# Second half's queries in two quarters that share one bank, and two key products next to the couples' loop

## The reference

```python
x = x + tanh(g_xattn[0]) * L0_xattn(layernorm(x), ctx, ctx)     # a decaying running sum
x = x + tanh(g_ffn[0])   * L0_ffn(layernorm(x), ...)            # 8 experts, 512 wide, 2 chosen
x = x + tanh(g_xattn[1]) * L1_xattn(layernorm(x), ctx, ...)     # 16 heads of 8, rotary, with biases
x = x + tanh(g_ffn[1])   * L1_ffn(layernorm(x), ...)            # 8 gated experts, 352 wide
x = x + tanh(g_xattn[2]) * L2_xattn(layernorm(x), ctx, ...)     # tanh(query + key) for all pairs, softmax
x = x + tanh(g_ffn[2])   * L2_ffn(layernorm(x), ...)            # 16 gated experts, 128 wide, 4 chosen
x = x + tanh(g_xattn[3]) * L3_xattn(layernorm(x), ctx, ctx)     # 16 heads of 8, rotary
x = x + tanh(g_ffn[3])   * L3_ffn(layernorm(x), ...)            # 8 experts and a shared one, 512 wide
```

## Time and profile before

| | us |
|---|---|
| median of three runs | 596.08 |
| the three runs | 593.05, 596.08, 596.30 |
| the profiled execution | 593.17 |
| its span, first to last instruction | 591.4 |
| TensorE busy in it | 559.5 (95%) |
| VectorE busy | 440.1 (74%) |
| ScalarE busy | 402.6 (68%) |
| GpSimd busy | 101.9 (17%) |

### The profile page before, as it was taken

How to read it: one execution, slowest core, us unless ns; L and a number is a source line. 1 busy time by engine, 2 the same in 40 slices (tenths; PEclk the granted TensorE clock), 3 DMA queues, 4 the chain that set the end, 5 groups by cost and what they waited for, 6 DMA issues and landing times.

```text
span 591.4 us, 8708 instructions
## 1 busy us (share of the span) xinstructions
PE 559.5 (95%) x3251; PEld 385.4 (65%) x3256; DVE 440.1 (74%) x684; ACT 402.6 (68%) x559; POOL 101.9 (17%) x69
## 2 busy tenths in 40 slices
PE   7999999889999999999996989999998999999997
PEld 5688887656777867764331437566545767888886
DVE  4378987678648799977789775766767838787786
ACT  4799899756746645426999865534504858888875
POOL 5400000000110000004989713100000310000000
PEclk9999999999999999999899899999999999999999
DMA  6208110300100559200000024406410110712100
GB/s 241 65 11 319 54 54 1 116 1 2 55 1 2 190 197 245 71 29 1 7 1 1 1 71 126 162 3 170 151 35 1 38 38 2 319 40 70 36 2 35
DMA packets 19342, 43.81 MB, mean 74 GB/s; under 512 B 2090, under 2 KB 7594, under 8 KB 19300
## 3 DMA queue, kind: packets, MB, share of 16 engines
q1 hardware_dynamic: 19300, 43.25, 22.8%
HBM read 42.55 MB, written 0.70 MB: 73 GB/s over the span
## 4 chain that ended last, share of the span: by engine, by line
PE 73%; DVE 14%; ACT 8%; issue 3%; POOL 1%; DVEq 0%; ACTq 0%; POOLq 0%
PE ps L801 36%; ACT work L1197 5%; PE ps L843 4%; PE ps L783 3%; PE ps L557 3%; PE ps L540 3%; DVE h_lo L1729 2%; PE ps L827 2%; PE ps L672 2%; PE ps L829 2%; PE ps L643 2%; PE ps L828 2%; PE ps L868 2%; PE ps L547 2%; PE ps L657 2%
## 5 line engine op out<-in xcount | busy, mean ns | idle before, releaser
L1729 DVE TENSOR_TENSOR h_lo<-h_act,h_hi 128x512 fp32r<-128x512 f32 (+1 forms) x114 | 103.5, 912 | 39.9 <-ACT h_hi L1244 39.1
L801 PE MATMUL ps<-n_hi,w_hi 128*128 128x512 f32 x224 | 86.5, 421 | 2.4 <-DVE h_act L1702 1.2
L1244 ACT CAST h_hi<-h_act 128x1024 fp32r<-128x1024 f32 (+1 forms) x88 | 75.3, 856 | 14.7 <-PE ps L801 12.1
L801 PE MATMUL ps<-n_hi,w_lo 128*128 128x512 f32 x224 | 79.7, 391 | 0.0
L801 PE MATMUL ps<-n_lo,w_hi 128*128 128x512 f32 x224 | 79.7, 390 | 0.0
L1943 POOL TENSOR_TENSOR rstd<-var_eps,minus_half 128x4 f32<-128x4 f32 x16 | 17.1, 1070 | 313.6 <-DVE var_eps L1389 313.6
L1197 ACT ACTIVATE work<-work,p_rest 128x2048 f32<-128x2048 f32 x31 | 59.4, 1995 | 0.4 <-DVE work L1582 0.4
L1237 ACT ACTIVATE h_act<-ps 128x512 f32<-128x512 f32 x44 | 26.3, 597 | 45.5 <-PE ps L801 45.2
L801 PE MATMUL ps<-h_hi,w_hi 128*128 128x512 f32 x162 | 56.3, 396 | 0.1
L801 PE MATMUL ps<-h_hi,w_lo 128*128 128x512 f32 x162 | 55.4, 390 | 0.0
L801 PE MATMUL ps<-h_lo,w_hi 128*128 128x512 f32 x162 | 55.4, 390 | 0.0
(11 more groups left out here) (239 smaller groups left out, 1036.0 us busy)
## 6 DMA issues: line engine op xcount, KB each, us to landing
work<-g_rows SPq DMA_DIRECT2D x36, 512.0 KB, 5.8
w_f<-in_w SPq DMA_DIRECT2D x20, 512.0 KB, 3.6
w_f<-in_w SPq DMA_DIRECT2D x8, 384.0 KB, 3.3
work<-g_rows SPq DMA_DIRECT2D x8, 256.0 KB, 6.9
work<-g_rows SPq DMA_DIRECT2D x4, 384.0 KB, 7.2
diag<-in_w SPq DMA_DIRECT2D x2, 512.0 KB, 4.8
work<-in_w SPq DMA_DIRECT2D x2, 512.0 KB, 4.5
w_f<-in_w_rest SPq DMA_DIRECT2D x2, 384.0 KB, 5.3
```

The costliest lines, as they stand in the source:

```text
L801: mm = pe.matmul(dst[i], wap(wt, e, lo, size, rows), mv[i], start=(first and c == 0), stop=(last and c == 2))
L1244: act.copy(places(h_hi, m, step), places(h_act, m, step)).then_inc(s["hi"], 1)
L1729: dve.tensor_tensor(lo, src, hi.bitcast(F32), ALU.subtract).then_inc(s["lo"], 1)
```

## The change

The second half's queries of both attentions are computed in two quarters of 256 tokens. A quarter's two products go to the left and the right half of bank 7. `query_rows` on VectorE and ScalarE then runs three times per attention in place of twice, and all its counts go by three. The second quarter's products come on TensorE in turn 1, its rotation on VectorE behind output(0), its mask on ScalarE behind the exponential of couple 2. The values of couple 0 no longer wait; turn_out(0) moves from turn 1 to turn 2, behind turn(2), and waits for the second quarter's rotation.

The two key products of layer 3's second half move out of steps 5 and 8 to behind the keep-busy products, of which 8 of 14 stay; the first goes to bank 4. ScalarE copies them behind hidden(0) and hidden(1). TensorE waits for these copies before out_bias(0) and before the first gate is spread. On VectorE the second hidden product moves from behind `weigh(1)` to between its two weighted sums.

```diff
-        KBANK = ({(t, r): 6 + r for t in range(2) for r in range(2)}, {(0, 0): 4, (0, 1): 4, (1, 0): 6, (1, 1): 6})
+        KBANK = ({(t, r): 6 + r for t in range(2) for r in range(2)}, {(0, 0): 4, (0, 1): 4, (1, 0): 4, (1, 1): 6})
-        QBANK, OBANK = (0, 6), (3, 7)
+        OBANK = (3, 7)
+        def queries_of(t):
+            return half(0) if t == 0 else slice(HALF + (t - 1) * HALF // 2, HALF + t * HALF // 2)
+        def query_bank(t, r):
+            return ps[:, r] if t == 0 else ps[:, 7, r * HALF // 2:(r + 1) * HALF // 2]
+        def query_part(p):
+            return 0 if p < HT else p // 2 - 1
...
# TensorE
-                        pe.wait_ge(pre["kcp"], 4 + 2 * t + r)
+                        pe.wait_ge(pre["kcp"], 4 + (r if t == 0 else 2))
...
-                pe.wait_ge(ln["n"], 2 * (2, 6)[i] + t + 1)
-                pe.matmul(ps[:, QBANK[t]], w[:, 0], n[:, half(t)], start=True, stop=True)
-                pe.matmul(ps[:, QBANK[t] + 1], w[:, 1], n[:, half(t)], start=True, stop=True).then_inc(at["q"], 1)
+                pe.wait_ge(ln["n"], 2 * (2, 6)[i] + min(t, 1) + 1)
+                if t == 2:
+                    pe.wait_ge(at["qT"], 3 * i + 2)
+                for r in range(2):
+                    mm = pe.matmul(query_bank(t, r), w[:, r], n[:, queries_of(t)], start=True, stop=True)
+                mm.then_inc(at["q"], 1)
...
-                    if p == 0:
-                        pe.wait_ge(at["qT"], 2 * i + 2)
...
+                    if p == 0:
+                        pe.wait_ge(at["qT"], 3 * i + 3)
                     pe.transpose(ps[:, 7, 0:P], ao[:, p % 2], ident).then_inc(at["aot"], 1)
...
                     turn(p)
-                    if p == 0:
-                        queries(i, 1)
+                    if p < 2:
+                        queries(i, 1 + p)
+                    if p == 2:
+                        turn_out(0)
                     if p + 2 < PAIRS:
                         scores(i, p + 2)
...
                     values(p)
-                    if p:
+                    if p >= 2:
                         turn_out(p - 1)
...
                     turn_gates((0,))
-                    keep_busy(14, 4)
+                    keep_busy(8, 4)
+                    prepare_keys(1, 1, 0)
+                    pe.wait_ge(once["gT"], nth(m))
+                    prepare_keys(1, 1, 1)
                     up(2)
+                    pe.wait_ge(pre["kcp"], 7)
                     out_bias(0)
...
                     up(10)
+                    pe.wait_ge(pre["kcp"], 8)
                     spread_gate(0)
...
-                    if L == 2 and step in (5, 8):
-                        prepare_keys(1, 1, (step - 5) // 3)
# ScalarE
-                    if p == 1:
-                        query_rows(i, 1)
+                    if p in (1, 2):
+                        query_rows(i, p)
...
                     hidden(0)
+                    copy_keys(1, 1, 0)
                     for e in range(4, 6):
                         split_hi_up(m, e)
                     hidden(1)
+                    copy_keys(1, 1, 1)
                     weights_tanh(1)
...
-                        if step in (19, 22):
-                            copy_keys(1, 1, (step - 19) // 3)
# VectorE
                     output(p)
+                    if p == 0:
+                        query_rows(i, 2)
...
-            def weigh(t):
+            def weigh(t, between=lambda: None):
                 for r in range(2):
+                    if r == 1:
+                        between()
...
-                    weigh(1)
-                    ahead()
+                    weigh(1, ahead)
```

More of the change, by code:

```diff
@@ L625, in queries @@
                     pe.wait_ge(mo[2 * i]["mul" if i else "act"], MOES[2 * i].total)
-                pe.wait_ge(ln["n"], 2 * (2, 6)[i] + t + 1)
-                pe.matmul(ps[:, QBANK[t]], w[:, 0], n[:, half(t)], start=True, stop=True)
-                pe.matmul(ps[:, QBANK[t] + 1], w[:, 1], n[:, half(t)], start=True, stop=True).then_inc(at["q"], 1)
+                pe.wait_ge(ln["n"], 2 * (2, 6)[i] + min(t, 1) + 1)
[4 more added lines that the diff above has]
+                mm.then_inc(at["q"], 1)
             def scores(i, p):
                 g = PAIRS * i + p
-                pe.wait_ge(at["q_rows_lo"], 2 * i + p // HT + 1)
-                pe.wait_ge(at["q_rows_hi"], 2 * i + p // HT + 1)
+                pe.wait_ge(at["q_rows_lo"], 3 * i + query_part(p) + 1)
+                pe.wait_ge(at["q_rows_hi"], 3 * i + query_part(p) + 1)
                 if p >= 2:
@@ L1093, in query_rows @@
             def query_rows(i, t):
-                act.wait_ge(at["qT"], 2 * i + t + 1)
-                act.activation(q_rows[:, 1, half(t)], qT[:, half(t)], ACT.Copy, scale=rmask[:, 1:2]).then_inc(at["q_rows_hi"], 1)
+                act.wait_ge(at["qT"], 3 * i + t + 1)
+                act.activation(q_rows[:, 1, queries_of(t)], qT[:, queries_of(t)], ACT.Copy, scale=rmask[:, 1:2]).then_inc(at["q_rows_hi"], 1)
             def expand_keys(i, t, h):
@@ L1398, in norm_low, with rotate @@
                 dve.tensor_tensor(n_lo[:, half(t)], n[:, half(t)], n_hi[:, half(t)].bitcast(F32), ALU.subtract).then_inc(ln["lo"], 1)
-            def rotate(dst, t, banks, tab, bias):
-                v = dst[:, half(t)].rearrange("p (b s) -> p b s", s=S)
-                tmp = ps[:, banks + 1].rearrange("p (b s) -> p b s", s=S)
+            def rotate(dst, t, tab, bias):
+                count = (queries_of(t).stop - queries_of(t).start) // S
+                v = dst[:, queries_of(t)].rearrange("p (b s) -> p b s", s=S)
+                src, tmp = (query_bank(t, r).rearrange("p (b s) -> p b s", s=S) for r in range(2))
                 b0 = abias[:, bias:bias + 1] if bias is not None else 0.0
                 b1 = abias[:, bias + 1:bias + 2] if bias is not None else 0.0
-                dve.scalar_tensor_tensor(v, ps[:, banks].rearrange("p (b s) -> p b s", s=S), b0, bcast(rope[:, tab], 1, 8), ALU.add, ALU.mult)
-                link(dve.scalar_tensor_tensor(tmp, tmp, b1, bcast(rope[:, tab + 1], 1, 8), ALU.add, ALU.mult))
+                dve.scalar_tensor_tensor(v, src, b0, bcast(rope[:, tab], 1, count), ALU.add, ALU.mult)
+                link(dve.scalar_tensor_tensor(tmp, tmp, b1, bcast(rope[:, tab + 1], 1, count), ALU.add, ALU.mult))
                 return dve.tensor_tensor(v, v, tmp, ALU.add)
@@ L1421, in query_rows @@
             def query_rows(i, t):
-                dve.wait_ge(at["q"], 2 * i + t + 1)
-                rotate(qT, t, QBANK[t], 0, 0 if i == 0 else None).then_inc(at["qT"], 1)
-                dve.wait_ge(at["qT"], 2 * i + t + 1)
-                dve.tensor_scalar(q_rows[:, 0, half(t)], qT[:, half(t)], rmask[:, 0:1], None, ALU.mult).then_inc(at["q_rows_lo"], 1)
+                dve.wait_ge(at["q"], 3 * i + t + 1)
+                rotate(qT, t, 0, 0 if i == 0 else None).then_inc(at["qT"], 1)
+                dve.wait_ge(at["qT"], 3 * i + t + 1)
+                dve.tensor_scalar(q_rows[:, 0, queries_of(t)], qT[:, queries_of(t)], rmask[:, 0:1], None, ALU.mult).then_inc(at["q_rows_lo"], 1)
             def attention(i):
```

## The result

| | before | changed |
|---|---|---|
| median of ten runs | 594.06 us | 590.01 us |
| lowest, highest | 592.39, 596.47 | 588.57, 593.35 |
| the profiled execution | 593.17 | 593.04 |
| its span | 591.4 | 591.3 |
| mean granted clock in it (1 is 2.4 GHz) | 0.994 | 0.988 |

The changed kernel takes 0.9932 of the time before, with a 95% interval of 0.9911 to 0.9952. That is 4.05 us less, between 2.9 and 5.3: faster by more than 0.5%, though the interval's near end (0.48%) lies just short of that bound. The forecast was a gain of 2.76 us and a time of 593.3, with a range of 589.6 to 595.8; the measured time lies in it, 0.4 us from its lower end.

The account below looks back on a forecast made before the run. It took TensorE to bound the kernel (73% of the last chain; VectorE 14%), with VectorE setting the attentions' gain. 1.17 + 1.72 - 0.13 = 2.76 us off the 596.08 median gave 593.3 us, range 589.6 to 595.8.

Parts of the forecast that it names:

- The edit to VectorE: Rotation and mask of one query quarter on VectorE: 1.62 us in the first attention, 1.51 in the second.
- The attentions' gain: Values of couple 2 start earlier in both attentions, VectorE setting the pace: 0.53 and 0.64 us, together 1.17.
- The first rival: In the attentions, VectorE's extra piece eats the gain; only the moved keys pay: 1.6 us, 594.5, chance 0.14.
- The second (TensorE sets the pace): In the attentions, the quarter's operations overlap more than summed, so TensorE sets the pace: 4.1 us, 592.0, chance 0.08.
- The shared bank: Both quarters' products in bank 7: no cost in this order, about 1.4 us of TensorE if issued back to back.
- The keys' gain: Two key products leave steps 5 and 8 of the third expert layer's loop: 1.72 us off TensorE's path.
- Behind the couples' loop: The second hidden product inside `weigh(1)` delays ScalarE and the update of x: 0.13 us lost, bounds 0 and 0.65.
- The sum: Whole kernel: attentions 1.17 plus keys 1.72 less 0.13 us for the moved hidden product, 2.76 us gained.
- The clock: TensorE's clock might fall in the changed stretches, a risk of loss; by the skill's rule, filled holes should keep it.
- The two forecast losses: One fall near the keep-busy products or an attention's start: 595.0, chance 0.11; a lasting 1.2 GHz: 600.3, chance 0.07.
- One of the signs: In the profile after, a granted clock under 1.0 in a stretch where it was full would show the forecast wrong.
- The anchor: Whole kernel: the gain was taken off the three runs' median, 596.08 us, not the profiled 593.17, giving 593.3.

Follow-up runs that it names:

- the quarters alone: The changed kernel with the key products back in steps 5 and 8, so only the attentions' part of the change stays; 593.32 us, ratio 0.9965.
- the kernel without the sine term: The changed kernel with two of three VectorE operations of the second quarter's rotation left out in each attention; 588.51 us, ratio 0.9895.
- the first one with the later quarter: The changed kernel with the second quarter's rotation behind output 1 instead of output 0, output turnings and ScalarE's copies moved too; 594.73 us, ratio 0.9991.
- the kernel with the copies behind the exponential: Against the kernel rotating the second quarter behind output 1: ScalarE's copy of output 0 put behind couple 3's exponential, output 1's later; 591.66 us, ratio 0.9947.

## Why the prediction was right, and where it was short

The mechanism held in each term of the sum; what the clock would do and the time that the sum was taken from did not. Both of these erred to the same side, and the measured time stayed within the range because its lower end had been taken from the faster of the three runs, with the larger gains below it.

**The edit to VectorE** was sized right: a quarter was put at 1.62 and 1.51 us and took 1.64 and 1.52. The widths for this came from other operations of the same kernel.

**The attentions' gain** was put at 0.53 + 0.64 = 1.17 us and was 0.56 + 0.67 = 1.23 (0.47 + 0.59 of it at the values of couple 2, for which it was forecast, and the rest in the couples behind them). The first rival (the extra piece eats it) fell by these rows and by the quarters alone. The second (TensorE sets the pace) fell by the holes of 1.04 and 0.80 us that VectorE releases. The prediction had TensorE 0.7 us early at these values; it was 1.04 early in the first attention. What it did not name is that ScalarE is only some half a microsecond behind VectorE there, by the profile of the kernel without the sine term.

**The shared bank** was costed at nothing in this order and at 1.4 us back to back. No wait for it is in the rows of the changed kernel, and back to back it made holes of 1.52 and 1.40, with 2.04 us for each attention in the end.

**The keys' gain** was put at 1.72 and was 1.79; neither the gates' transfers nor VectorE's work came late enough to take it back. **Behind the couples' loop** 0.13 us lost were forecast and 0.08 measured. The cover held: the idle time before the next step is 1.23 us where about 1.2 were expected. The mean of the updated x is 13.8 us behind the start of the keep-busy products (347.60 to 361.40), not 13.5, since these products start 0.22 us earlier against the softmax than before.

**The sum** of 2.76 us was 2.94 by the profiles and 3.0 by the spans at equal clock. So the structural part was short by 0.2 us.

**The clock** is the step that failed. It stood in the prediction only as a risk of loss (chance 0.11 and 0.07), and the gain that it held possible (filled holes keep the clock) was given no term in the sum. Measured, the mean granted clock rose from 0.9904 to 0.9934, worth 1.1 to 1.7 us. Together with 3.0 this is 4.1 to 4.7, beside 4.05 in the first table and 4.7 between the medians of all 76 and 16 executions. The two forecast losses did not come: the stretches behind the loop and in the attentions ran at 1.00 in both profiles of the changed kernel. One of the signs that the prediction named for being wrong did appear, a granted clock under 1.0 where it had been full: 0.76 to 0.81 from 8 to 16 and 0.57 from 324 to 328. The change does not touch these stretches, so the sign was too wide; it does not speak against the sum.

**The anchor** failed as well. The prediction hung its sum on the median of the three runs shown, 596.08, although the profiled execution (593.17) stood 2.9 us below. Ten runs beside the changed kernel had a median of 594.06, and 76 over the whole study 594.86. Of the 3.3 us between forecast and measured time, 2.0 are this anchor and 1.3 the gain that was short. That two of the three runs came from the slower end was bad luck, not a step of the reasoning.

**Why the clock rises stays open.** Both parts seem to raise it, by 0.0013 and 0.0016, though neither figure is clear of chance by itself. The falls near 288 and 332, which all three profiles of before have, lie in stretches that the change does not touch. One of the two profiles of the changed kernel has both, the other neither; of the ten profiles of kernels with the quarters or the moved keys four have the first and four the second. In exchange six of the ten have a fall from 8 to 16, which none of the three has. So the falls move far away from the edits, and no filled hole has been tied to one. A fall at the start of the second attention (448 to 456) is in one of the profiles of before and in that of the quarters alone, but in none of the changed kernel. Against the reading that the filled holes of the attentions do it stand the kernel with both quarters back to back, with more holes and 0.9941, and the first one with the later quarter, with a hole of 1.92 us and 0.9929. The rule that the clock follows how busy TensorE has been (the Trainium skill, TensorE: Matmul & The Clock Gate, What's actually happening) fits the direction of the whole change, but not these two kernels. With one or two profiles for each kernel, the places of single falls cannot be counted.

## What to carry to other kernels

When idle time in front of one step is bought with more work on the engine that releases it, follow that engine to the next step that it releases: here 1.45 us of holes went and 1.04 us came back two couples later, and the gain was the difference in the releasing engine's own schedule. A shared bank was free where other work covered the reading of its first use (here the second pair of products came 4.06 us behind the first), and cost 2 us an attention where none did. Before comparing two kernels that differ by half a per cent, set spans of equal mean granted clock beside each other: two profiles that agree within 0.1 us hid a gain of 3 us here. Such groups are good to about 1 us, so small differences still want the offsets of single instructions.

## What the runs showed of the hardware

The granted clock of TensorE falls to 1.2 GHz for a few microseconds at a time. In the profiles this happens near 8 to 16, 288, 316 to 336 and 448 us, at places that change in part from execution to execution of the same program: the three profiles of before share 288 and 332 and one adds 448. A profile with one such fall has a mean clock of 0.997, one with two 0.994, one with three or four 0.991 and 0.988, so by the mean clocks of 1.000 to 0.985 there are none to five in an execution. A fall near 588, behind the last matmul, is not in these mean clocks and costs nothing: in the profiled execution of the changed kernel the offset is -0.13 us at the last products and -0.1 at the end. Each of the others costs about 1.1 to 1.7 us between the groups (1.41 and 1.65 us by the offsets of two of them), so that executions of one kernel fall into clusters at that distance, and for the kernel before a straight line through the mean clock accounts for 87% of the variance of its spans, whose times run from 592.4 to 598.1 us. In the couples' loop these falls came behind stretches in which TensorE was busy only in part: in the profiled execution of the changed kernel 2.34 and 2.04 of 4 us from 316 to 324. But the kernel before was busy 2.35 and 2.04 there and had no fall at 324, and the kernel with the copies behind the exponential was busy 2.53 of 4 us from 284 to 288, as the kernel before was, and had no fall at 288. So the busy time of the stretch ahead does not by itself tell whether a fall comes. A small change of the program shifts how often each cluster is drawn; the shift here was worth about half as much as the 3.0 us that the change saves at equal clock.

A single fall can also be long: behind a hole of 2.89 us with few matmuls around it TensorE ran at 1.2 GHz from about 351.5 to 362, which cost 3.05 us. In this stretch the keep-busy products (1.9 us of them, or 3.0 before) guard against something that came in one profile out of one without them, and in none of the twelve with them; the median of the times does not show their worth.
